# A separate first transfer of two channels, and sixteen matmuls on a tile of ones ahead of the first product

## The reference

```python
def _gn(v, G=32, eps=1e-5):                       # group norm, two channels to a group
    g = v.reshape(B_, G, C_ // G, H_, W_)
    return ((g - mean(g)) / sqrt(var(g) + eps)).reshape(v.shape)

res = conv3x3(x, W_id, b_id)                      # of all 8 images
cA, cH, cV, cD = _swt2_level3(x[0])               # wavelet maps of image 0 alone
low_att  = _attention(cA[None], DCT_LOW,  W_dl, ...)
high_att = _attention(stack(cH, cV, cD), DCT_HIGH, W_dh, ...)
out = leaky_relu(conv3x3(concat(low_att, high_att), W_enc, b_enc), 0.01)
return x + out + res                              # x inside the block is _gn(x)
```

## Time and profile before

| | us |
|---|---|
| median of 3 runs | 2002.18 |
| lowest and highest | 2000.6, 2009.61 |
| the profiled execution | 2005.66 |
| its span, first to last instruction | 2003.5 |
| TensorE busy in it | 1960.9 (98%) |
| VectorE, ScalarE, GpSimd busy | 1490.2, 975.9, 1025.5 |

### The profile page before, as it was taken

One profiled execution on the slowest core, in us unless ns is written; L12 is line 12 of the kernel. 1 busy time (PEld: TensorE's weight loads), 2 busy tenths in 40 slices (PEclk: granted clock), 3 DMA queues, 4 the chain that ended last, 5 costly groups with the idle time before them and its releaser, 6 DMA issues.

```text
span 2003.5 us, 79772 instructions
## 1 busy us (share of the span) xinstructions
PE 1960.9 (98%) x35664; PEld 1616.3 (81%) x35664; DVE 1490.2 (74%) x2310; ACT 975.9 (49%) x1003; POOL 1025.5 (51%) x769
## 2 busy tenths in 40 slices
PE   8999899999999999999999999999999999999998
PEld 7897799999999999866667787786687667877784
DVE  5765478778777777577777777777777777777776
ACT  3433466666666666644444444444444344444442
POOL 0003678887888787444444444444444444444444
PEclk9999899999999999999999999999999999999999
DMA  7952677888788886488887888787878877878874
GB/s 168 288 220 65 197 182 199 217 211 216 202 214 218 204 209 150 94 207 201 205 201 195 202 204 205 203 203 196 199 201 206 204 201 194 201 202 205 207 201 125
DMA packets 132251, 391.92 MB, mean 196 GB/s; under 512 B 49622, under 2 KB 50388, under 8 KB 118068
## 3 DMA queue, kind: packets, MB, share of 16 engines
q1 hardware_dynamic: 131940, 387.09, 75.7%
HBM read 258.56 MB, written 128.45 MB: 193 GB/s over the span
## 4 chain that ended last, share of the span: by engine, by line
issue 32%; PE 31%; POOL 25%; POOLq 1%; ACT 1%; DVE 0%; DVEq 0%; ACTq 0%
POOL stage L1553 25%; PE ps L1016 14%; PE ps L991 7%; PE ps L995 5%; PE ps L994 3%; POOLq L1551 1%; PE ps L1004 1%; DVE shared L1186 0%; DVE pool_of L1192 0%; ACT pool_of L1384 0%; ACT pool_of L1379 0%; ACT shared L1101 0%; POOL big L1257 0%; ACT big L1071 0%; DVE pool_of L1145 0%
## 5 line engine op out<-in xcount | busy, mean ns | idle before, releaser
L1553 POOL TENSOR_TENSOR stage<-stage,big 128x448 f32<-128x448 f32 x448 | 510.7, 1140 | 645.7 <-DVE stage L1528 642.9
L1465 PE MATMUL ps<-pool_of,w_hi 64*64 64x448 f16 x12096 | 648.6, 350 | 8.2 <-issue 8.0
L1465 PEld LDWEIGHTS ps<-pool_of,w_hi 64*64 64x64 f16 x12096 | 443.2, 107 | 160.2 <-issue 13.1
L1465 PE MATMUL ps<-pool_of,w_lo 64*64 64x448 f16 x8064 | 454.6, 350 | 0.7 <-issue 0.7
L1465 PEld LDWEIGHTS ps<-pool_of,w_lo 64*64 64x64 f16 x8064 | 301.7, 107 | 100.5 <-issue 2.6
L1528 DVE SCALAR_TENSOR_TENSOR stage<-ps,w_max,pool_of 64x448 f32<-64x448 f32 x448 | 305.9, 683 | 47.1 <-PE ps L1465 34.4
L1528 DVE SCALAR_TENSOR_TENSOR stage<-ps,w_max,xs 64x448 f32<-64x448 f32 x384 | 262.2, 683 | 34.4 <-PE ps L1465 22.8
L1157 DVE BATCH_NORM_STATS2 pool_of<-big 128x6 f32<-128x448 f32 x392 | 232.3, 616 | 68.1 <-DMA big<-in_x 68.0
L1379 ACT ACTIVATE pool_of<-pool_of 128x2240 f16<-128x2240 f32 x56 | 126.4, 2258 | 314.8 <-PE ps L1465 314.8
L1379 ACT ACTIVATE pool_of<-xs,pool_of 128x2240 f16<-128x2240 f32 x48 | 108.4, 2258 | 285.7 <-PE ps L1465 285.7
L991 PE MATMUL ps<-pool_of 112*128 112x246 f16 x1344 | 222.7, 275 | 10.3 <-DVE pool_of L1194 5.4
(11 more groups left out here) (188 smaller groups left out, 2527.7 us busy)
## 6 DMA issues: line engine op xcount, KB each, us to landing
out<-stage SPq DMA_DIRECT2D x448, 224.0 KB, 3.1
big<-in_x SPq DMA_DIRECT2D x392, 224.0 KB, 5.1
pool_of<-in_x SPq DMA_DIRECT2D x104, 560.0 KB, 7.0
xs<-in_x SPq DMA_DIRECT2D x96, 560.0 KB, 7.3
pool_of<-row_filtered SPq DMA_DIRECT2D x110, 224.0 KB, 3.6
row_filtered<-big SPq DMA_DIRECT2D x3, 6272.0 KB, 21.7
pool_of<-in_x SPq DMA_DIRECT2D x32, 392.0 KB, 7.0
row_filtered<-big SPq DMA_DIRECT2D x1, 4928.0 KB, 20.6
```

What stands on the lines that cost most here:

```text
L1465: mm = pe.matmul(psum[4 * p + 2 * g + r][C * k:C * k + C, 0:NT], w[lanes, t, :], v[lanes, y:y + 2, kx:kx + W], start=(j == 0), stop=(j == ...
L1553: pool.tensor_tensor(stage[p][:, r, g, :], stage[p][:, r, g, :], e_map[:, e:e + NT], ALU.add)\
```

## The change

The two transfers of group 0 become four: channels 0 and 1 in two transfers that signal a new semaphore `pair_in`, then channels 2 to 7 in two that signal `group_in[0]`. All other groups are loaded as before. TensorE waits for `ones` to be set, multiplies it by itself 16 times into bank 7, where nothing reads it, and then goes on; channel 0 now waits for `pair_in`, channel 2 for `group_in[0]`. VectorE's first statistics wait for both.

```diff
                 def load(k):
                     wc, g = k // NGR, k % NGR
-                    for hc in range(2):
-                        src = x[0, g * CG:g * CG + CG, hc * HALF:hc * HALF + HALF, wc * HALF:wc * HALF + HALF]
-                        sp.dma_start(xg[g][:, hc, :, :], src.rearrange("c h w -> h c w")).then_inc(group_in[g], 16)
+                    for a, b, signal in ((0, 2, pair_in), (2, CG, group_in[0])) if k == 0 else ((0, CG, group_in[g]),):
+                        for hc in range(2):
+                            src = x[0, g * CG + a:g * CG + b, hc * HALF:hc * HALF + HALF, wc * HALF:wc * HALF + HALF]
+                            sp.dma_start(xg[g][:, hc, a:b, :], src.rearrange("c h w -> h c w")).then_inc(signal, 16)
...
+                pe.wait_ge(ones_set, 1)
+                for k in range(16):
+                    pe.matmul(small[:, 0:P], ones[:, :], ones[:, :], start=True, stop=True)
                 pe.wait_ge(fh_in, 16)
...
-                        if hh == 0 and c % CG == 0:
+                        if n == 0:
+                            pe.wait_ge(pair_in, 32)
+                        elif n == 2 or hh == 0 and c % CG == 0:
                             pe.wait_ge(group_in[g], 32 * wc + 32)
...
                     if c == 0:
                         dve.wait_ge(group_in[g], 32 * wc + 32)
+                        if k == 0:
+                            dve.wait_ge(pair_in, 32)
```

More of the change, by code:

```diff
@@ L335, in before_maps @@
         fh_in = sem(s1, "fh_in")
+        pair_in = sem(s1, "pair_in")
         group_in = [sem(s1, f"group_in{i}") for i in range(NGR)]
```

## The result

| | before | changed |
|---|---|---|
| median, us | 2002.18 | 1998.95 |
| lowest and highest of 17 runs | 1997.49, 2009.61 | 1991.43, 2002.3 |
| the profiled execution, its span | 2005.66, 2003.5 | 1998.68, 1996.7 |

The ratio is 0.9977 with a 95% interval of 0.9966 to 0.9988: 4.6 us faster (2.4 to 6.8), 3.2 us by the medians.

A forecast was written before the change was run, and what follows sets the result against it. TensorE, busy 98% of the span, was taken as the bound. A gain of 3.4 us, 2.5 from pace and the rest from an earlier start, took the median from 2002.18 to 1998.8 us; range 1994.5 to 2004.0.

The forecast's parts named there:

- The end of the ones, 6.9: At the start: 16 matmuls on ones, 0.43 us each at half pace, 0.22 at full, end at 6.9 us.
- rival B: Ones at the start: weight loads not hidden, 0.85 or 0.43 us a matmul, end 10.3; gain 0, 2002.2 us; chance 0.12.
- The moment of the rise, 3.5 to 4.6 us after the first matmul: During the ones: TensorE goes from half to full pace; either value changes the sum by at most 0.3 us.
- The rest of group 0, 8.2: Image load, channels 2 to 7: lands at 8.2 us, 0.3 later than before; bounds 7.8 and 8.7.
- Pass 1 at 46.45: End of pass 0: 62 channels at 0.617 us after 8.2; pass 1 at 46.45, not 49.82, gain 3.4 us.
- Passing to the end: After pass 0: write, load and restart come earlier by as much, the 4.6 us wait stays; gain carried undiminished.
- Rival A: Second wait, in pass 1: grows from 4.6 to 8.0 us and gives the gain back; 2002.2 us; chance 0.10.
- Rival C: Ones at the start: unhidden and clock left low, end 14.75, pass 0 ends at 56.7; 2009.1 us; chance 0.05.
- Case D: Later half-pace stretches, at 77 and 144 us, come out otherwise: 2 to 5 us either side, about 1995 to 2003; chance 0.15.

The follow-up runs named there:

- ones alone: The kernel before plus only the sixteen matmuls on ones, image loaded as before; median 1999.7 us, ratio 0.9988.
- four and four: The changed kernel with group 0 split into channels 0 to 3 and 4 to 7, second wait at channel 4; median 1998.59 us, ratio 0.9986.
- pair alone: The changed kernel without the matmuls on ones, keeping the separate transfers of channels 0 and 1; median 2003.11 us, ratio 1.0012.

## Why the prediction was right, step by step

- **The end of the ones, 6.9.** 6.28 and 7.55 in the two profiles: the value lies between, 0.6 us from either. The price of one was right: 0.214 us a record, 0.43 a matmul, at half pace. At full pace the 32 records in pass 1 took 56.66 - 53.07 = 3.59 us, 0.112 each and 0.22 a matmul, as forecast. At half pace a record of 14 moving columns and one of 128 take the same 0.214 us, so load and stream lie over each other, and rival B fell, whose prices were 0.43 and 0.85 a matmul. The rule of the Trainium skill that stood for B ("TensorE: Matmul & The Clock Gate", "The mechanism", the section ahead of the one that the prediction names) does not hold for these float32 records, all on one set of 112 rows. The forecast's nearest row, line 505, has 64 rows and not 112, so it is the same in columns alone.
- **The moment of the rise, 3.5 to 4.6 us after the first matmul.** This term was too narrow. Under the ones of 128 columns it was about 3.3 to 3.8 us in three profiles (changed, ones alone, 32 ones) and 5.5 to 6 in three others (changed and ones alone a second time, four and four). The forecast tried 3.5 and 4.6 and found the sum moved by no more than 0.3 us by either; a later rise was not reckoned with. In the second profile it put the end of the ones at 7.55 and channel 2 at 8.79, 0.6 later than the forecast's 8.2. The pace of the products was full from channel 0, as forecast.
- **The rest of group 0, 8.2.** 8.8 in the first profile, where it was the limit, and 8.2 in the second, where it was none. The other kernels with the pair have 8.2, 8.1, 8.0 and once 9.4. So the value was good and the upper bound of 8.7 was not; a landing after 8.7 and a wait of over 1 us at channel 2 are what the prediction named as wrong in size, and the first profile has both (8.8, 1.1). Group 0 of the ones alone, with no transfer added, landed at 8.7 and 8.4 where the profiles of before have 7.9, 7.8 and 7.5: the ones delay it by themselves, a term that the forecast did not have. Its 0.3 us were for two issues.
- **Pass 1 at 46.45.** 47.12 and 47.02, 2.70 and 2.80 us ahead of the earlier trace rows and 2.45 ahead of the mean of three profiles, in place of 3.4. In the first profile the late landing makes the difference, in the second the late rise of the pace. Either puts pass 1 some 0.6 us later than forecast; the other 0.3 us lie in the profile that the forecast started from, whose pass 1 was that much later than the mean.
- **Passing to the end.** Right as far as the restart: 27.17 and 27.32 us from pass 1 to it, 27.16 to 27.22 before. Rival A fell; the ones in pass 1 show where it would have held. That the gain passes from there to the end undiminished is not shown, since the scatter behind the restart covers it.
- **Rival C** did not come. Of its two conditions, 14 moving columns show one: the pace stays at half, and pass 1 came at 50.58. The other, loads that are not hidden (0.85 a matmul, pass 1 at 56.7), was met in no run. What the forecast held against it, 128 moving columns a load, is what made the difference.
- **Case D.** Right in kind and size: 5.2 us between two executions of one program. The measured 1998.95 agrees with 1998.8 to 0.2 us, and that is luck: the gain at the start was 1 us less than forecast, and the interval is 4.4 us wide. 2.5 us are shown at the start, the medians have 3.2, and the interval 2.4 to 6.8. Whether the rest is D or a further effect of the change stays open.

## What to carry to other kernels

Before pricing an earlier start, find the first wait downstream that TensorE doesn't set, and see what it is tied to: here a shift ahead of its trigger passed whole, and a shift behind it vanished. What a filler moves matters: 16 matmuls of 128 columns had the first product at full pace, 16 of 14 columns had not, though both kept TensorE busy. Their number costs as soon as they outlast the data. Where one effect is a thousandth of the time, compare milestones of several profiles; the time of one execution says nothing.

## What the runs showed of the hardware that I had not expected

- **Being busy did not bring full pace by itself.** After sixteen matmuls of 128 columns the first product was at full pace, at 6.28 us at the earliest; sixteen that took 6.85 us without a gap but moved 14 columns left it at half pace to about 14.
- **The early transfers are slower when the start is changed.** 262 to 266 GB/s in four profiles with the start as it was, 228 to 239 in nine and 255 in one with ones, or smaller first transfers, or both. The engines' share is 1.19 to 1.20 either way, but for one 1.15. What does it isn't known.
- **The rise is late and varies.** From the first product 4.5 us, 3.5 to 5.6 in the four profiles with the start as it was, near 7 with the pair alone; from the first of the ones 3.3 to 6 with 16 or 32 of them; with 11 ones and a pause it came near 10, 9 us after the first of them. The clock column showed 1.00 throughout, at half pace too, as in the earlier trace rows.
- **How long TensorE could idle and keep its pace.** After 1.29 and 2.01 us idle the next product was at full pace; after 4.6 it was at half, at a granted clock of 0.50.
- **A short filler in front of a long wait may pay.** With 16 matmuls in pass 1 the granted clock behind the restart was 1.00, and that kernel's gain over before (0.9978) was like the changed one's (0.9977). That the filler's effect on the pace is the whole cause is not shown.
